# ScalarE's order for a routed group: the two Silus of the next group stand ahead of the loads four groups ahead

## The reference

```
x = layernorm(x + mamba(x))
h = silu((x_n @ w1[e])) @ w2[e]     # x_n: RMS norm of x, times rms_w[e]; hidden width 256
x = layernorm(x + sum of the 2 best of 14 routed experts, weighted by the softmax gates
                + sum of 2 shared experts)
```

## Time and profile before

| what | value |
|---|---|
| runs | 769.2 us median of 3 (768.94 to 770.51) |
| profiled execution | its span is 769.2 us |
| busy in the span | PE 651.3 us (85%), DVE 596.1 (77%), POOL 501.3 (65%), ACT 444.7 (58%) |
| loads issued by ACT | 77 of 64.5 KB, from 584.1 to 719.4 us |
| returns by POOL | 141, from 481.1 to 749.3 us |

### The profile page before, as it was taken

One profiled execution on the slowest core, in us unless ns is written; L12 is line 12 of the kernel. 1 busy time (PEld: TensorE's weight loads), 2 busy tenths in 40 slices (PEclk: granted clock), 3 DMA queues, 4 the chain that ended last, 5 costly groups with the idle time before them and its releaser, 6 DMA issues.

```text
span 769.2 us, 14716 instructions
## 1 busy us (share of the span) xinstructions
PE 651.3 (85%) x4299; PEld 554.7 (72%) x4299; DVE 596.1 (77%) x1744; ACT 444.7 (58%) x1225; POOL 501.3 (65%) x545
## 2 busy tenths in 40 slices
PE   5987798999999999999999997965988878767830
PEld 4765576788888888888888886854987768656720
DVE  4999999999999999999999864427447343698875
ACT  4885688867877876787787543411223111346445
POOL 1144565887797897888888776556655656566561
PEclk9999999999999999999999998878889889997865
DMA  8541111211221121111111055114222236536126
GB/s 305 193 138 42 43 43 41 64 57 55 62 64 62 60 62 50 63 64 60 59 50 62 22 167 192 45 55 101 80 80 77 76 80 172 168 100 205 60 80 218
DMA packets 62638, 70.76 MB, mean 92 GB/s; under 512 B 10335, under 2 KB 45285, under 8 KB 62304
## 3 DMA queue, kind: packets, MB, share of 16 engines
q1 hardware_dynamic: 41568, 47.70, 19.6%
q0 software_dynamic: 8608, 16.87, 6.5%
q10 hardware_dynamic: 12384, 5.26, 2.9%
HBM read 48.55 MB, written 23.01 MB: 93 GB/s over the span
## 4 chain that ended last, share of the span: by engine, by line
PE 60%; DVE 13%; issue 12%; ACT 7%; another core or an unknown queue 4%; ACTq 2%; DMA 1%; DVEq 0%; SPq 0%
PE bank L745 7%; PE bank L817 6%; PE bank L826 6%; PE bank L884 6%; PE bank L770 5%; PE bank L800 5%; DVE xbcT_area L1155 3%; PE bank L881 3%; PE bank L871 3%; PE bank L833 3%; PE bank L785 3%; PE bank L888 2%; DVE decay_area L1163 2%; ACT x L933 2%
## 5 line engine op out<-in xcount | busy, mean ns | idle before, releaser
L623 POOL DMA_INDIRECT returned<-xT,slots_in x141 | 142.1, 1008 | 107.6 <-DVE xT L1453 67.3
L669 POOL DMA_INDIRECT dispatched<-rows,row_u x128 | 143.7, 1123 | 33.9 <-issue 31.8
L745 PE MATMUL bank<-xT 128*128 128x128 f32 x564 | 92.0, 316 | 43.4 <-issue 24.9
L1155 DVE SCALAR_TENSOR_TENSOR xbcT_area<-raw,conv_w,xbcT_area 128x512 f32<-128x512 f32 x162 | 123.9, 766 | 2.9 <-ACT xbcT_area L999 2.9
L745 PEld LDWEIGHTS bank<-xT 128*128 128x128 f32 x564 | 82.7, 226 | 50.7 <-issue 42.4
L944 ACT ACTIVATE raw<-bank 128x512 f32<-128x512 f32 (+1 forms) x71 | 39.8, 590 | 126.9 <-remote 61.5
L661 POOL TENSOR_TENSOR state_kept<-state,whole 128x256 f32<-128x256 f32 x56 | 72.1, 1288 | 59.0 <-DVE state L1181 49.1
L1453 DVE COPY xT<-bank 128x512 f32<-128x512 f32 (+1 forms) x36 | 24.3, 676 | 90.5 <-remote 72.8
L770 PE MATMUL bank<-xbcT_area,raw 128*128 x564 | 83.4, 308 | 4.7 <-issue 4.6
L1163 DVE TENSOR_TENSOR_SCAN decay_area<-decay_area,ident_heads 128x512 f32<-128x512 f32 x64 | 85.0, 1329 | 0.0
L770 PEld LDWEIGHTS bank<-xbcT_area,raw 128*128 128x128 f32 x564 | 79.6, 224 | 7.0 <-issue 7.0
(11 more groups left out here) (228 smaller groups left out, 1497.0 us busy)
## 6 DMA issues: line engine op xcount, KB each, us to landing
decay_area<-decay_rows SPq DMA_DIRECT2D x64, 256.0 KB
slots_in<-dispatched ACTq DMA_DIRECT2D x77, 64.5 KB
hid<-returned SPq DMA_DIRECT2D x18, 256.0 KB
slots_in<-dispatched SPq DMA_DIRECT2D x64, 64.5 KB
xT<-xT_dram SPq DMA_DIRECT2D x8, 512.0 KB, 7.9
x<-x_dram SPq DMA_DIRECT2D x8, 512.0 KB, 7.8
out_dram<-x SPq DMA_DIRECT2D x16, 256.0 KB
xT<-returned SPq DMA_DIRECT2D x14, 256.0 KB
```

Source lines behind the costliest of these rows:

```text
L623: e.indirect_dma_start(returned, bass.IndirectOffsetOnAxis(ap=slots_in[sb_][:, n, D:ROW].bitcast(U32), axis=0), slots_out[b][:, n * P:(n + ...
L669: e.indirect_dma_start(dispatched, bass.IndirectOffsetOnAxis(ap=row_u[t % 2][:, m:m + 1], axis=0), rows[t % 3][:, k, c4, :], None).then_in ...
L745: mm = e.matmul(bank[:, off:off + P], w1_now[b][:, k * P:(k + 1) * P], slotsT[gr % len(slotsT)][:, n % 4 * P:(n % 4 + 1) * P], start=True, ...
L1155: e.scalar_tensor_tensor(o, r[:, n:n + W], conv_w[:, k, TAPS - 1 - n:TAPS - n], o, ALU.mult, ALU.add).then_inc(S["conv"])
```

## The change

In ACT's loop over groups 11 to 35 the call that takes the Silus of group gr+1 is put ahead of the block that loads group gr+4. Nothing else is touched; the same instructions run on every engine, and PE's, DVE's, POOL's and SP's streams are the same.

```
@@ -1045,6 +1045,8 @@
                     e.activation(pick_v[:], pick_v[:], ACT.Exp).then_inc(S["gate_exp"])
 
+                if gr + 1 < GROUPS:
+                    routed_silu(gr + 1)
                 ahead = gr + 4
                 if LOADED_BY_ACT <= ahead < GROUPS:
                     on.wait_ge("dispatched1", (NT // 2) * 8 * 16)
@@ -1055,8 +1057,6 @@
                     if ahead % 2 == 0:
                         first_rows = rows_of(ET.Activation, ahead)
                     load_slots(e, ahead, first_rows)
-                if gr + 1 < GROUPS:
-                    routed_silu(gr + 1)
                 s = tail_step(gr)
                 if s is not None:
                     by_token(s)
```

## The result

| | median | range | runs |
|---|---|---|---|
| before | 769.59 us | 765.09 to 772.98 | 20 |
| changed | 773.53 us | 769.22 to 777.64 | 20 |

The ratio is 1.005, with a 95% interval of 1.0033 to 1.0067. The change costs 3.9 us (2.5 to 5.2). The forecast of 769.8 us is missed, and the time lies outside the range as well.

A forecast was written before the change was run, and what follows sets the result against it. From iteration 23 DVE was taken to carry the path, with the time set by its copy of group 35 plus about 21 us. Terms 0 + 0.5 + 2.1 - 2.0 + 0 = +0.6 us on 769.2 gave 769.8 us, range 767.0 to 772.6.

The forecast's parts named there:

- Part 1: Iterations 12 to 21: every load comes about one group later, Silus start as before; costed at nothing.
- Part 2: Iteration 22: load 26 now stands ahead of set 0's scaling, delaying DVE's add; +0.5 us, between 0 and 0.7.
- Part 3: Iteration 24: load 28 behind a late Silu delays set 2's scaling and DVE's add; +2.1 us, between 0 and 2.1.
- Part 4: Iterations 25, 27, 29: Silus directly follow the norms, so DVE waits less for ACT; -2.0 us, between 0 and -2.0.
- Part 5: Iterations 26, 28, 30: even loads behind Silus that wait for PE just fit; costed at nothing.
- rival A: Even loads behind late Silus delay the scaling in iterations 26, 28 and 30 too; 772.2 us, chance 0.28.
- Rival B: Late Silu release at 671.21 us goes, load 28 issues early, iteration 24 loses nothing; 767.7 or 767.2 us, chance 0.20.

The follow-up runs named there:

- e17: Kernel before with Silus ahead of the load in iterations 12 to 21 only: median 767.83 us against 766.92, ratio 0.9995 (0.9965 to 1.0026).
- e8: Kernel before with Silus ahead of the load in all iterations but 19 to 21, on a 718 us chip: 715.94 us, ratio 0.9973.
- e7: The whole change, with SP's first fetches of returned rows held until PE has turned group 24, on a 718 us chip: 715.54 us, 0.9972 of before.
- e16: Kernel before with Silus ahead of the load in iterations 22 to 31 only: 767.05 us against 766.39, ratio 1.0015 (0.9982 to 1.0049).
- e12: Kernel before with Silus ahead of the load only in iterations 25, 27, 29 and 31: 772.15 us, ratio 1.0036.
- e14: Silus first in odd iterations from 25, plus two short POOL memsets between second and third return of odd groups from 25: 762.82 us, 0.9959 of before.
- e4: Kernel before with Silus ahead of the load in iterations 22 to 31 only, on a 718 us chip: 714.90 us, ratio 0.9958.
- e6: The kernel of e4 measured again, on a 718 us chip: 716.85 us against 717.99 for before, ratio 0.9973.
- e18: The whole change plus two POOL memsets in the middle of every group's returns from group 12 on: 761.04 us, 0.9926 of before.
- e15: Kernel before plus two POOL memsets in the middle of every group's returns from group 12 on: 762.05 us, ratio 0.9954.

## Why the prediction was wrong

*Part 1 (iterations 12 to 21, nothing):* not settled. Its reasoning had a hole: I called the load of group 26 the tightest, with 2.5 us to spare, and it was that of group 24 which came late, though it was asked for 7.7 us ahead. The wait of 4.21 us at turn 24 reached copies 22 and 23, each of which comes 1.8 us later behind the one ahead of it than in the first profile of before. e17 bounds the loss at 2.0 us, but its profile lacks that wait. e8, without the wait, and e7, with 2.5 us of it, have the same ratio, and both ran on a 718 us chip.

*Part 2 (+0.5):* not seen. The scaling of set 0 started at 657.42 and DVE added at 658.84 without a wait. Copy 22 was late itself there, and it was not tried alone.

*Part 3 (+2.1, the largest term):* the delay of 2.8 us behind a Silu is there, the wait of DVE is not, since the release was early in this profile. In e16, with the same order there, the scaling starts at 664.70, 2.7 us behind the Silu, and DVE adds set 2 at 669.05 without a wait. I had taken the upper bound, and nothing shows that it was ever paid.

*Part 4 (-2.0):* **this step failed.** It said that iterations 25, 27 and 29 gain 2.0 us; alone, in e12, they cost 2.6 us (ratio 1.0036, 1.0013 to 1.006). The forecast shortening happened: DVE's wait went from 1.02 to 0.44 us. But I let copy 26 follow DVE's own work. I had read "DVE carries the path" from its busy time and from the lack of a wait at the copy, and never asked how near the copy's other input was. PE's product had been told in time with a stop in POOL's run, and that stop came from the wait I was glad to see go; without it the signal came 0.9 us behind the run, and with one put in by hand (e14) at once. The sum had -1.0 us for the sets 3 and 5; the step between the copies grew by 0.96 us twice instead. On the 718 us chips, where neither copy waits for PE, the same term holds: 0.63 us at the step looked at, and 0.4 and 0.3% in all (e4, e6).

*Part 5 and rival A:* the sign of A came true, and 773.5 us is near its 772.2, but by luck: its mechanism didn't. The even loads don't bite: DVE waits for ACT at neither set 4 nor set 6 in the changed profile, and the odd iterations alone cost 2.6 us. Rival B's early release did come, without its gain.

*The range* ended at 772.6 since every term was bounded by ACT's and DVE's rows. POOL's run was seen as what delays a signal (rivals A and B), but how DVE's add stretches POOL's returns, and what that does to the next signal, was in no term.

Of e12's 2.6 us, 1.9 are shown as longer steps, and with a stop on POOL (e14) these steps are short again. How the whole change's 3.9 us divide stays open. e18 shows that the stops take the loss back, but they stand in every group from 12 on, and so don't tell iterations 12 to 24 from those behind. The changed kernel's own profile has 0.8 us more from copy 25 to 28 and 2.3 us more from copy 12 to 25; e17 leaves up to 2.0 us for iterations 12 to 21 and e16 up to 3.8 us for 22 to 31. Not run: the whole change but 19 to 21 on a chip of this kind, and stops in groups 25 to 31 alone with before's order.

## What to carry to other kernels

A wait can do work: before taking one away, look at what its delay keeps apart on the other engines, above all on one whose instructions the later work lengthens. For each instruction that shows no wait, ask how long before its start its other inputs were there; those with the least room set the price of going earlier. And where the copies sit on late signals from another engine, spreading a run of indirect transfers can be worth as much as reordering around them: two memsets per group (0.5%) gained as much as this change does on the chips that like it (0.4%).

## What the runs showed of the hardware

*POOL's return waits for DVE's add.* Over the profiles, a return that starts a time t after the start of an add (tensor_tensor of two SBUF tiles, 0.69 us) takes about 1.54 us less t as long as t is under 0.57 us: 1.40 at 0.14, 1.26 at 0.28, 1.19 at 0.35, 1.03 at 0.50, and 0.97 at 0.68. So the return is held until 0.57 us after the add's start, 0.12 us before the add's recorded end, and then takes its whole 0.97 us. The Trainium skill (SBUF — State Buffer, Who interferes with whom) says that a DVE instruction with two SBUF inputs contends with a GpSimd instruction that reads SBUF; these rows agree as far as the add holds the return. The other way round nothing shows: all 288 such adds of the eighteen profiles with four returns take 0.69 us, those that start during a return too.

*PE's signal comes late behind POOL's runs of indirect transfers, on the 766 to 770 us chips.* In e12 PE's product that by the model ended at 685.9 us raised its semaphore at 688.11, 0.9 us after the end of POOL's fourth return. On a 718 us chip (e4) every copy from 13 on that DVE waited for starts within 0.05 us of the modelled end of PE's product, with POOL returning no less densely. Why the chips differ, and where the signal stands in the meantime, no run here shows. Behind groups 25 and 27 the next signal is in time with a spacing of 1.70 us or more (six profiles) and late with 1.56 (one) or 1.28 us (three, the changed one in part); this is seen, not explained. It is no rule for the whole stage: the stops of e15 and e18 space the second and third return as widely in every group from 12 on, and copy 23 of e15 and copy 24 of e18 still wait 3.02 and 5.52 us.
